# Moving work between engines in a recurrent mixer: join reads on ScalarE, scaling and clearing on GpSimd, joins over all rows

## The reference, cut to what matters

```python
mixed = silu(conv4(hidden @ W_qkv.T))            # q, k: 8 heads, repeated to 16; v: 16 heads
z     = hidden @ W_z.T
beta  = sigmoid(hidden @ W_b.T)
g     = -exp(A_log) * softplus(hidden @ W_a.T + dt_bias)
def step(S, (q, k, v, g, b)):                    # over the 114 tokens
    S  = S * exp(g)
    kv = einsum('bhkv,bhk->bhv', S, k)
    S  = S + k[..., None] * ((v - kv) * b[..., None])[..., None, :]
    return S, einsum('bhkv,bhk->bhv', S, q)
h_ = o * silu(z)
h_ = h_ * rsqrt(mean(h_ * h_, -1) + EPS) * norm_weight
out = h_ @ W_out.T
```

## Time and profile before

| | |
|---|---|
| median of 3 runs | 2999.57 us (2992.38 to 3015.68) |
| the profiled execution | 3003.69 us |
| its span, first to last instruction | 3001.8 us |
| busy: PE, DVE, ACT, POOL | 2500.1, 2091.0, 1251.3, 779.5 us |
| TensorE's mean granted clock | 0.873 of full speed |

### The profile page before, as it was taken

The page is one execution under the profiler, slowest core; times in us unless marked ns, Lnnn a source line. Parts: engine busy times, 40 slices in busy tenths (PEclk is TensorE's granted clock), DMA queues, the critical chain, the costliest instruction groups (busy, mean ns, idle before and its releaser), DMA issues. The chain is left out here.

```text
span 3001.8 us, 53659 instructions
## 1 busy us (share of the span) xinstructions
PE 2500.1 (83%) x19286; PEld 1924.7 (64%) x19286; DVE 2091.0 (70%) x4972; ACT 1251.3 (42%) x2990; POOL 779.5 (26%) x612
## 2 busy tenths in 40 slices
PE   7999989994579999999999999885652947889798
PEld 6777768874457777777777777664441825666454
DVE  5888863334588998998989899862662436886663
ACT  1444441121555665666666566532100313444132
POOL 2111100001132323222222222210676056450110
PEclk9999999995778998998999899887665967899799
DMA  4310002004112211121212222111212942110000
GB/s 145 99 42 29 14 3 60 22 23 157 32 47 50 50 48 42 42 51 39 48 40 49 51 50 50 47 44 56 83 34 56 298 127 59 43 51 1 23 21 25
DMA packets 274345, 169.00 MB, mean 56 GB/s; under 512 B 182847, under 2 KB 250318, under 8 KB 273728
## 3 DMA queue, kind: packets, MB, share of 16 engines
q1 hardware_dynamic: 247949, 140.28, 16.5%
q0 software_dynamic: 26112, 25.03, 3.2%
HBM read 99.23 MB, written 73.45 MB: 58 GB/s over the span
## 5 line engine op out<-in xcount | busy, mean ns | idle before, releaser
L1780 PE MATMUL d_ps<-d_xT,w_qkv 128*128 128x228 f32 x1024 | 222.6, 371 | 24.7 <-DMA d_xT<-normed_t 24.1
L1780 PEld LDWEIGHTS d_ps<-d_xT,w_qkv 128*128 128x128 f32 x1024 | 201.5, 199 | 58.1 <-DMA d_xT<-normed_t 25.7
L1288 POOL TENSOR_TENSOR qd<-decay,qm 114x456 f32<-114x456 f32 x128 | 146.0, 1160 | 259.1 <-DVE qm L1373 258.2
L1555 ACT ACTIVATE decay<-d_ps,gates 114x114 f32<-114x114 f32 x512 | 140.4, 362 | 161.0 <-DVE nt L1386 64.7
L1346 DVE TENSOR_TENSOR ue<-ue,elim_tmp 128x30 f32<-128x30 f32 (+14 forms) x480 | 194.3, 405 | 16.5
L1301 POOL TENSOR_SCALAR_AFFINE_SELECT ue<-ue 128x1024 f32<-128x1024 f32 x16 | 86.2, 5384 | 448.5 <-DMA ue<-blocks_n 448.5
L2495 POOL DMA_INDIRECT s_eo<-rows_y,slots_all x128 | 152.4, 1191 | 148.8 <-POOLq L87 110.8
L1344 DVE TENSOR_TENSOR elim_tmp<-ue 128x30 f32<-128x30 f32 (+14 forms) x480 | 170.8, 356 | 20.8 <-issue 8.5
L1421 DVE SCALAR_TENSOR_TENSOR y_v<-raw,taps,y_v 128x228 f32<-128x228 f32 x384 | 180.7, 544 | 5.5 <-ACT y_v L1593 5.3
L1768 PE MATMUL d_ps<-gl,after 114*114 114x456 f32 x256 | 132.0, 599 | 61.1 <-ACT gl L1566 37.2
L1421 DVE SCALAR_TENSOR_TENSOR y_qk<-raw,taps,y_qk 128x228 f32<-128x228 f32 x384 | 145.7, 449 | 22.5 <-ACT y_qk L1593 22.0
(11 more groups left out here) (341 smaller groups left out, 5618.4 us busy)
## 6 DMA issues: line engine op xcount, KB each, us to landing
rows_x<-zero_row SPq DMA_DIRECT2D x4, 2048.0 KB
ue<-blocks_n SPq DMA_DIRECT2D x16, 512.0 KB, 4.8
blocks_u<-ue SPq DMA_DIRECT2D x16, 512.0 KB, 2.8
blocks_v<-on SPq DMA_DIRECT2D x16, 512.0 KB, 2.9
e_x<-rows_x SPq DMA_DIRECT2D x32, 256.0 KB, 4.2
e_gu<-L_ffn_w_gate_up SPq DMA_DIRECT2D x32, 256.0 KB, 4.2
rows_y<-e_y SPq DMA_DIRECT2D x32, 256.0 KB, 3.3
blocks_n<-nt SPq DMA_DIRECT2D x96, 64.0 KB
```

Of the source, the lines that this page charges most:

```text
L1288: pool.tensor_tensor(qd[p.par][s][:, hs(u), :].rearrange("p (a o b) t -> p a o b t", o=2, b=2)[:, :, o], e[o][:, :, :].rearrange("p (a b) ...
L1555: last = act.activation(e[o][:, m, :], ps[0:S, 4 + o, m * S:(m + 1) * S], ACT.Exp, bias=gates[:, bass.ds(p.sample(s), 1), head:head + 1].r ...
L1780: last = pe.matmul(ps[:, f % 2, (t % 2) * W:(t % 2 + 1) * W], w_qkv[:, k, t * 128:(t + 1) * 128], xT[:, k, :], start=(k == 0), stop=(k == ...
```

## The change

1. `join_read` moves from VectorE to ScalarE, between `rhs_read` and the other reads.
2. `gate_scale` moves from VectorE to GpSimd, behind each `gate_power`.
3. A join takes all 114 rows of `nt` and `x` instead of 32, and both pairs are done in one call, alternating. So do `substitute` for the upper half and `carry`. For this everything in `x` that isn't a loaded block must be zero: GpSimd clears `x` (two memsets of 114x1024, `clear_x`) before the blocks are loaded, and after the joins it clears the blocks of rows 64 to 96 (`clear_gap`, two memsets of 32x512), which `substitute` waits for.
4. `w_z`, `gain` and `w_out` are loaded at the start of the mixer instead of in `prepare`, and `w_z` is halved there, between the first and the second turn.
5. The order of the calls in a turn is new on PE, DVE, ACT and POOL. The head of VectorE no longer holds the two scalings and the second residual; `conv(nxt, 0, 1)` comes before the first `gate_silu`; `first_tap` 0 and 1 on ScalarE come before the joins.

```diff
-                    for dst, src in (
-                        (w_qkv[:, :, :], dr["L0_attn_W_qkv_t"].rearrange("(k p) n -> p k n", p=128)),
...
-                        (w_z[:, :, :], dr["L0_attn_W_z_t"].rearrange("(k p) n -> p k n", p=128)),
...
+                    sp.dma_start(w_qkv[:, :, :], dr["L0_attn_W_qkv_t"].rearrange("(k p) n -> p k n", p=128)).then_inc(mix_in, 16)
+                    sp.dma_start(taps[:, :, :], dr["L0_attn_conv_w_c"]).then_inc(mix_in, 16)
...
-                ch(dve.tensor_scalar(w_z[:, :, :], w_z[:, :, :], 0.5, None, ALU.mult))
...
+            if between:
+                between()
...
-                        need(sp, o_mm, r.n * 4)
+                        sp.wait_ge(x_clear, r.n * 2 + 2)
...
+                sp.dma_start(w_z[:, :, :], dr["L0_attn_W_z_t"].rearrange("(k p) n -> p k n", p=128)).then_inc(wz_in, 16)
+                for dst, src in (
+                    (gain[0:DH, :], dr["L0_attn_norm_weight"].unsqueeze(1)),
+                    (gain[DH:128, :], dr["L0_attn_norm_weight"].unsqueeze(1)),
+                    (w_out[:, 0:4, :], dr["L0_attn_W_out_t"].rearrange("(k p) n -> p k n", p=128)[:, 0:4, :]),
+                    (w_out[:, 4:8, :], dr["L0_attn_W_out_t"].rearrange("(k p) n -> p k n", p=128)[:, 4:8, :]),
+                ):
+                    sp.dma_start(dst, src).then_inc(wo_in, 16)
...
+                def clear_x(r, s):
+
+                    need(pool, o_mm, r.n * 4 - 2 + 2 * s)
+                    pool.sem_inc(pool_gate, 1)
+                    pool.memset(x[s][:, :, :], 0.0).then_inc(x_clear, 1)
...
+                def clear_gap(r, p, done, a, d, products, powers, scales):
+
+                    rows, _, o = JOINS[1]
...
+                    for s in range(2):
+                        pool.wait_ge(zz_mm, r.n * 4 + 2 * s + 2)
+                        pool.sem_inc(pool_gate, 1)
+                        pool.memset(x[s][rows, :, o:o + BW], 0.0).then_inc(x_gap, 1)
+                    pool.wait_ge(x_gap, r.n * 2 + 2)
+
+                def gate_scale(r, s):
+                    pool.wait_ge(rms_r, r.n * 2 + s + 1)
+                    pool.tensor_tensor(on[s][:, :].rearrange("p (h d) -> p h d", h=H), sz[s][:, :].rearrange("p (h d) -> p h d", h=H),
+                                      bcast(ms[s][:, :], DH), ALU.mult).then_inc(on_r, 1)
...
-                def join_read(r, m):
-                    s, g = CHAINS[m]
-                    dve.wait_ge(zz_mm, r.n * 4 + m + 1)
...
-                    if d:
-                        gate_scale(done, 0)
...
+                def scale_gate():
+                    dve.wait_ge(wz_in, 16)
+                    dve.tensor_scalar(w_z[:, :, :], w_z[:, :, :], 0.5, None, ALU.mult).then_inc(wz_r, 1)
...
+                def join_read(r, m):
+                    s, g = CHAINS[m]
+                    act.wait_ge(zz_mm, r.n * 4 + m + 1)
+                    need(act, ww_mm, r.n * 4 - 3 + m)
+                    for _, rows, _ in JOINS:
+                        last = act.copy(zs[s][rows, hs(g), :], ps[rows, XBANK[m], 0:256].rearrange("p (h c) -> p h c", h=8))
+                    last.then_inc(zs_r, 1)
...
-                    lower, rows, o = JOINS[n]
-                    for i in range(8):
-                        last = pe.matmul(ps[rows, XBANK[m], i * BW:(i + 1) * BW], nt[r.par][s][lower, 8 * g + i, rows],
-                                         x[s][lower, 8 * g + i, o:o + BW], start=True, stop=True)
-                    last.then_inc(zz_mm if n else za_mm, 1)
...
+                    for i in range(8):
+                        for _, rows, o in JOINS:
+                            last = pe.matmul(ps[rows, XBANK[m], i * BW:(i + 1) * BW], nt[r.par][s][:, 8 * g + i, rows],
+                                             x[s][:, 8 * g + i, o:o + BW], start=True, stop=True)
+                    last.then_inc(zz_mm, 1)
...
-                        last = pe.matmul(ps[rows, XBANK[m], i * DH:(i + 1) * DH], ut[s][known, 8 * g + i, rows],
-                                         x[s][known, 8 * g + i, :], start=True, stop=True)
+                        last = pe.matmul(ps[rows, XBANK[m], i * DH:(i + 1) * DH], ut[s][:, 8 * g + i, rows],
+                                         x[s][:, 8 * g + i, :], start=True, stop=True)
...
-                        last = pe.matmul(ps[HALVES[1], VBANK[m], i * DH:(i + 1) * DH], nt[r.par][s][HALVES[0], 8 * g + i, HALVES[1]],
-                                         x[s][HALVES[0], 8 * g + i, :], start=False, stop=True, skip_group_check=True)
+                        last = pe.matmul(ps[HALVES[1], VBANK[m], i * DH:(i + 1) * DH], nt[r.par][s][:, 8 * g + i, HALVES[1]],
+                                         x[s][:, 8 * g + i, :], start=False, stop=True, skip_group_check=True)
...
```

More of the change, by code:

```diff
@@ L924, in _, with prepare @@
                     last.then_inc(o_mm, 1)
-def prepare(c, hid, xts, gates, w_qkv, w_z, w_out, taps, gain, qmask):
+def prepare(c, hid, xts, gates, w_qkv, taps, qmask):
     nc, dr = c.nc, c.dram
@@ L1148, in delta_net @@
         taps, gain, qmask = sb("taps", [128, CT, TAPS]), sb("gain", [128, 1]), sb("qmask", [S, S])
-        c.stage(prepare, hid, xts, gates, w_qkv, w_z, w_out, taps, gain, qmask)
+        c.stage(prepare, hid, xts, gates, w_qkv, taps, qmask)
         xT, xz = sb("d_xT", [128, KD, W]), sb("d_xz", [128, KD, W])
@@ L1295, in gate_power @@
                     pool.tensor_tensor(ms[s][:, :], ms[s][:, :], c.minus_half[0:S, :], ALU.pow).then_inc(rms_r, 1)
+                def clear_gap(r, p, done, a, d, products, powers, scales):
+                    rows, _, o = JOINS[1]
+                    if a:
+                        need(pool, qd_r, p.n * 8 + products)
+                    if d:
+                        need(pool, rms_r, done.n * 2 + powers)
+                        need(pool, on_r, done.n * 2 + scales)
+                    pool.wait_ge(x_clear, r.n * 2 + 2)
+                    for s in range(2):
[7 more added lines that the diff above has]
+                                      bcast(ms[s][:, :], DH), ALU.mult).then_inc(on_r, 1)
                 def mask_blocks(p):
@@ L1438, in iteration @@
                     if z:
-                        eliminate(r, 1, 2)
+                        eliminate(r, 1, 5)
+                    if a:
+                        query_mask(p, 0)
+                        weights(p, 0)
+                        weights(p, 1)
+                    if z:
+                        eliminate(r, 5, 6)
                     if d:
@@ L1608, in oT_read @@
                 def oT_read(r, s):
+                    if isinstance(r.n, int) and r.n == 0:
+                        act.wait_ge(wo_in, 64)
                     need(act, wo_mm, r.n * 2 + s)
@@ L1644, in iteration @@
                         decay_exp(p, 0)
+                        decay_exp(p, 1)
                     if d:
                         gate_squares(done, 1)
+                    if a:
+                        decay_terms(p, 2)
                     if proj:
@@ L1650, in iteration @@
                     if a:
[L1651 removed]
+                        decay_exp(p, 2)
                         decay_terms(p, 3)
[L1653 removed]
+                        decay_terms(p, 4)
                     if proj:
@@ L1684, in iteration @@
                     if proj:
+                        raw_read(nxt, 5)
                         decay_terms(nxt, 0)
-                        raw_read(nxt, 7)
+                        first_tap(nxt, 0)
+                        raw_read(nxt, 6)
+                        first_tap(nxt, 1)
+                    if d:
+                        oT_read(done, 1)
+                    if a:
+                        decay_exp(p, 7)
                     if z:
                         gate_tanh(r, 0)
-                    if a:
-                        decay_exp(p, 7)
                     if proj:
-                        first_tap(nxt, 0)
+                        raw_read(nxt, 7)
                     if z:
@@ L1787, in gate_product @@
                     if n == 0:
+                        if isinstance(r.n, int) and r.n == 0:
+                            pe.wait_ge(wz_r, 1)
                         pe.wait_ge(xz_in, r.n * 16 + 16)
@@ L1810, in output_product @@
                 def output_product(r, s):
+                    if isinstance(r.n, int) and r.n == 0 and s == 0:
+                        pe.wait_ge(wo_in, 64)
                     pe.wait_ge(oT_r, r.n * 4 + 2 * s + 2)
@@ L1910, in iteration @@
                         decay(p, 0)
+                        products(p, 0)
+                        decay(p, 1)
                     if proj:
@@ L1914, in iteration @@
                     if a:
-                        decay(p, 1)
-                        products(p, 0)
                         decay(p, 2)
@@ L1919, in iteration @@
                         project(nxt, 2)
+                    if a:
+                        products(p, 1)
+                        decay(p, 3)
```

(2 more changed lines are left out.)

231 lines of the change are left out of this document (89 added, 142 removed).

## The result

The changed kernel takes **2904.4 us** (median of 4 runs, 2896.3 to 2908.2) against 2999.7 for the kernel before in the same session: a ratio of **0.967 [0.963, 0.972]**. The forecast was 2932, with a range of 2870 to 3006. The direction and the main mechanism (the clock of the tail) came out as told; the head got shorter where it was forecast to get longer. The gain is 95 us where 68 were forecast. Ratios here leave out executions over 1.5% longer than the fastest of their kernel, and the profiled executions of the first two experiments (3152.3 and 3027.0 us) are such long ones.

A forecast was written before the change was run, and what follows sets the result against it. VectorE bounds the head, DRAM the hop, TensorE and its clock the tail. 15 turns x (5.1 - 0.8) = 64.5; 3003.7 - 64.5 - 6 + 2 = 2935 profiled, median 4 us below, given as 2932 us; range 2870 to 3006.

The forecast's parts named there:

- the main mechanism: Tail: with products on 114 rows TensorE's clock stays at 2.4 GHz nearly always, tail 32.3 to 27.2 us.
- What bounds the kernel: One turn: VectorE sets the head (37.0 us), DRAM the hop (8.3 us), TensorE the tail (31.6 us), which depends on the clock.
- The rows term: Tail: joins, upper substitution and carry on 114 rows keep the clock up; new tail 27.2 us, gain 5.1 us a turn.
- Rival A: Tail: the clock doesn't follow the rows, low stretches come from TensorE's pauses before the joins; tail stays 32.3, 3008 us; chance 0.15.
- The 0.9 us left for turns still at the low clock: Tail: average allowance for turns with a low clock somewhere, three tenths of carry's 3.14 us difference; 26.3 becomes 27.2 us.
- The join reads' cost of 1.1 us: Tail: with join reads on ScalarE, TensorE waits 0.7 us before substitution, plus 0.4 us for later meetings.
- The scaling term: Head: moving two scalings to GpSimd saves VectorE 2.6 us but holds it 3.4 us; net +0.8 us a turn.
- the sign of the head: Head: forecast to get longer, by 0.8 us a turn, with bounds -2.6 and +2.4.
- rival C: Head: scalings find VectorE at PSUM work, so it loses its 2.6 us; tail 26.3 us, total 2867 us; chance 0.13.
- Clearing: GpSimd memsets, 2 us a turn in the head and 1.1 us in the tail, cost nothing; between nothing and 2 us considered.
- Late weights: End of `prepare`: 2 of 4 MB of weights leave, ScalarE's wait and the `w_z` halving shrink; -6 us, bounds 0 and -8.
- The end: Two last turns: VectorE has little else to do and a scaling takes 2.5 instead of 1.23 us; +2 us.

The follow-up runs named there:

- the first two experiments: Changed kernel with joins on 32 rows in two parts, upper substitution and carry on 64: 3084.8 us, 1.021; with only substitution and carry on 64 rows: 2984.1 us, 0.991.
- The second attempt: Changed kernel with its ten loop turns written out and both scalings back on VectorE, behind eliminations 10 and 15: 2882.2 us, 0.956 to the kernel before.

## Why the prediction was right, and where it was not

*What bounds the kernel*: right. A head of VectorE, a hop of DMA, a tail of TensorE with the clock as its price; the experiments moved the time through one of these or through what lies ahead of the mixer.

*The rows term*, 15 x 5.1 = 76.5 us: right, also in size. The tails lost 77.8. Its starting point (the last turn with joins, 25.9 us at 1.00) was a fair model of every turn. The rows alone gave 0.976 on the old kernel, and undoing those of substitution and carry took the new one from 0.967 to 0.991. Rival A (the clock doesn't follow the rows) is out as the main cause: the hop, with TensorE's pause in it, is 8.2 us on average before and after. One reading was loose: in the turn of the earlier trace rows the clock falls 1.5 us into the joins (1429.9 and 1431.4 in the earlier trace rows), not behind them.

*Its parts* were less good. The 0.9 us left for turns still at the low clock came out nearly right by luck. It was priced by carry's 3.14 us, though a low stretch slows every form in it; and it was left for the wrong thing, as of the 15 tails one has a low stretch, 3.4 us:

```profile
1096.94 1.04 PE L1904 MATMUL d_ps<-upd,nt 114*50 114x64 f32 x15 [2.65 <-issue]
...
1099.18 2.92 PE L1904 MATMUL d_ps<-upd,nt 114*50 114x64 f32 x29
```

The fall comes behind a pause of 2.65 us, for which the profile names no releaser, and carry then takes 2.92 us where it took 2.01. This tail is 4.4 us over 26.3, 0.3 a turn on average. Shorter pauses of this kind, 0.4 to 1.6 us in six other tails at 1.00, add about 0.4 a turn. What they are is open.

The join reads' cost of 1.1 us (TensorE waits 0.7 and 0.4) looks like the hole of 1.03 us in the timeline, but taking the reads off ScalarE gives 0.3 to 0.7: there the tap of 1.61 us still stands just ahead of the read into `ut`, and the hole is still 0.76 us in the turn looked at.

*The scaling term was mis-sized, and with it the sign of the head*: the failed step. Forecast +0.8 us a turn, measured -1.05 in a quiet turn (35.69 to 34.64) and -0.47 on average. VectorE lost the 2.28 us of scaling and 0.33 of a residual, as forecast. Against it I had held 3.4 us, 4/5 of 2 x 2.15. From start to start, the 60 instructions of elimination take 25.1 us in a quiet head before and 26.6 after, so the net of all holds grew by 1.5 us. Two things make the difference. First, in a quiet turn one scaling holds a whole instruction, by 1.58 to 1.75 us (the instruction starts up to 0.45 us behind it), and the other falls on the mask and the weight and costs 0.34 to 0.50 us on the elimination behind them. I had spread the holds by the share of time, but in a fixed order each scaling falls on the same place in every quiet turn. That is half of rival C. Second, the sum left out the new order. What `query_decay` adds to eliminations in a quiet head, by their durations above the usual for their shape, fell from 3.3 to 1.7 us. So the -1.05 us is not the scaling's alone. The second attempt has the new order on both sides and confirms the sign: +0.8 us a head with the scaling back on VectorE.

*Clearing*: forecast nothing, bounds 0 to 2 us a turn. The memset beside eliminations costs nothing, as told, but in the ten heads not behind a jump the one beside the mean's `TENSOR_SCALAR` holds it for 0.97 to 1.08 instead of 0.17 us, and the elimination behind it ends about 0.67 us late. The Trainium skill (SBUF — State Buffer, Who interferes with whom) says that `tensor_scalar` can enter a two-port mode and then contends with GpSimd. The trace agrees; I had applied only the page's rule on instructions with two SBUF inputs, and a second rule of the page spoke of this instruction. That it is the memset, and not the end of `query_decay` just ahead of it, two heads of the kernel with join reads on VectorE and the loop show: there `query_decay` had ended before, the `TENSOR_SCALAR` came 0.36 and 0.39 us into the memset, and took 0.62 and 0.60 us, to 0.03 us behind the memset's end.

*Late weights*, -6 us: right (5.4 us off the wait, 5.8 us to the first elimination, 6.4 when undone). Over all profiled runs the first elimination starts at 831.5 to 835.6 us with the late loads and at 839.6 to 843.5 without.

*The end*, +2 us: not seen. From the last copy to the end of the span there were 974.7 us before and 969.0 after, and 966.9 to 983.2 in the twelve other profiled runs, so neither the 5.8 us gained there nor a loss of 2 can be told from what comes and goes.

*What no step had*: the four heads behind a jump, 3.8 us longer than the others, 15 us in all. Before, a jump cost its gap and little else; the new order put VectorE's first demand on TensorE closer to the turn's start than the jump's low clock allows. The first head's 4.65 us on the other side had no step either: it waited 3.14 us for TensorE before.

The sum: heads 22.7 us better than forecast (12 forecast as a loss, 10.7 gained), the end 7.8 better, tails 1.3 better, hops and gaps 2.4 worse, the weights 0.2 worse. That makes 29 us, the distance from 2935 to the profiled 2906. Of these only the heads are a finding; the 7.8 us of the end lie within what other executions show.

## What to carry to other kernels

When many small products stand in a row, look at the granted clock per stretch before counting instructions: the same number of products on more rows, with the surplus rows cleared, was worth 2.4% here. When an instruction moves to GpSimd, ask which VectorE instruction it will fall on in the fixed order, not what share of them can be held. An order that suits a quiet turn can be fragile just behind a loop's jump: the heads there, 38.6 us for 34.8, are worth a look of their own, and writing the loop out gave another 1%.

## What the runs showed of the hardware that I had not expected

- TensorE at 0.50 for 40.6 us with 40.45 us busy, the last 19 of them on 114 rows (rows undone): a busy engine alone did not raise the clock there.
- A loop's jump left VectorE of the changed kernel without an instruction for 2.4 to 2.65 us, and each of the four goes with 3.4 to 6.8 us of TensorE at 0.50. In the kernel with join reads on VectorE one jump of 2.58 us passed at 1.00.
- With full rows, eight falls of the clock inside tails each came behind a pause of TensorE of 1.6 to 2.9 us and lasted 3.4 us.
- A `TENSOR_SCALAR` of 16 elements a row took 0.99 us beside a GpSimd memset and 1.33 to 1.57 us beside a GpSimd scaling (masks asked for later), for 0.17 alone, where a two-input elimination beside another memset lost nothing.
